# One transformer layer on eight cores: an earlier weight load, two input loads on another queue, an earlier reload for the second half, and a down projection moved behind the next chunk

## The chip, the cores and the metric

The kernel runs on one Trainium2 chip. It is one program on all 8 cores; each core takes one of the 8 sequences of the batch and computes the whole layer for it. The cores exchange nothing. The metric is the device time in microseconds of the slowest core.

## What is computed

One layer, post-layernorm: linear attention with a gate, then a mixture of 16 experts with a shared expert, each followed by residual and layernorm. Per core: 2048 tokens of width 1024, all float32.

```python
q = elu(x @ Wq + bq) + 1;  k = elu(x @ Wk + bk) + 1;  v = x @ Wv + bv     # 16 heads of 64
kv   = einsum('bhsd,bhse->bhde', k, v)          # one 64x64 matrix per head, over all 2048 tokens
attn = q @ kv
h    = layernorm(x + (sigmoid(x @ Wg + bg) * attn) @ Wo + bo)
c    = top-4 of 16 gate weights of softmax(h @ gate_w.T), within the best 2 of 4 groups
y    = sum over experts e of c[:, e] * ((silu(h @ w1[e]) * (h @ w3[e])) @ w2[e])    # inner width 512
z    = (silu(h @ ws1) * (h @ ws3)) @ ws2                                            # inner width 1024
out  = layernorm(h + y + z)
```

## The kernel before

Every float32 operand of a large matmul is split in two bf16 parts (hi and lo), and each product is three matmuls, hi x hi, hi x lo and lo x hi, which the helper `mm3s` (lines 238 to 243) issues. So all large matmuls stand at lines 239, 241 and 242, whatever they compute.

The program is a list of operations per engine (`Sched`, lines 51 to 85), unrolled in full. Each operation has waits on semaphores (an engine's counter and a value), each engine runs its list strictly in order, and a DMA is started by the engine in whose list it stands: "sy" is SyncE (the trace's SPq), "gp" is GpSimd (POOL), "se" is ScalarE (ACT). `Sched.add` drops a wait that the same engine has already made with at least that value.

Stages, in order of time:

- Phase A (lines 263 to 357), 16 tiles of 128 tokens: k and v, and their product kv in PSUM. Then kv is copied out of PSUM on VectorE (line 365), cast on ScalarE (369), and its low part computed on VectorE (370).
- The weights of phase B, Wq, Wg, Wo (386 to 403), in 12 chunks through the single staging buffer `wstage`: DMA on SyncE's queue (390), cast to hi on ScalarE (397), lo part on GpSimd (399). The next chunk's load waits for the lo part of the one before. The first chunk's load waits for `barA`, the last operation of phase A on TensorE, VectorE and ScalarE.
- Phase B (441 to 639), 8 chunks of 256 tokens: load x (445, SyncE's queue, two loads of 512 KB into one of two buffers `xb`), transpose (458), q, g, attention, Wo, residual, layernorm, h written to DRAM (`h_scr`, and transposed as `hth_scr` and `htl_scr`). The x loads of chunks 0 and 1 stand in SyncE's list behind the twelve weight loads.
- Phase C (726 to 1095), two halves `hh` of 1024 tokens. Each half: 16 loads of the transposed h (732, 736), zero `acc` (740), router (757 to 859), 16 experts (861 to 970) with weights staged by `load_split_slot`, then the shared expert, then the layernorm `LN` (1062 to 1092).

Shared expert: its weights ws1, ws3, ws2 come in 12 chunks through `wstage` (972 to 990): load on SyncE's queue (977), a copying DMA on GpSimd's queue for the hi part (983), the lo part on GpSimd (986). For each group of 512 tokens (`tg` 0 and 1) it runs over 8 inner chunks `ic` (994). Each `ic` is 24 + 24 matmuls for h1 (ws1) and h3 (ws3), then silu on ScalarE (1013), product on VectorE (1017), cast (1021) and low part (1025). After `ic` 3 and after `ic` 7 the down projection of the four chunks just made follows: 96 matmuls with ws2 into PSUM banks 4 to 7, eight results of 512 columns, each added to `acc` on VectorE (1052). Here y0 is the one after `ic` 3 and y1 the one after `ic` 7. The buffer `aT` holds four chunks only, so `ic` 4 may write it only after y0 has read it.

LN, eight tiles of 128 tokens: load of h on ScalarE's queue into the single buffer `hln` (1063), residual on VectorE (1066), sums and scaling (1071 to 1086), output written by a DMA that stands in GpSimd's list (1090). For the second half the lists go on: SyncE's has the 16 loads of the transposed h (they wait for `pe_gate`, all of TensorE's work of the first half), then the first expert's weights; GpSimd's has the eight output DMAs of LN ahead of the first expert's copying DMA (718) and lo part (720); VectorE's has LN ahead of the zeroing (740) and of the router's copies (777).

Of the kernel before, what the change touches and what calls it, by code (L numbers as in the profile page):

```python
# [22 lines left out]
ALU = mybir.AluOpType  # L23
# [64 lines left out]
def build_program():  # L88
    nc = bass.Bass("TRN2", target_bir_lowering=False)

    xin = nc.dram_tensor("x", [S, D], F32, kind="ExternalInput").ap()
# [22 lines left out]

    Sd = Sched()
    for nm in ("PE", "VE", "SE", "GP", "GPD", "LDI", "LDB", "XA0", "XA1", "WA",
               "XB0", "XB1", "WB", "HW", "HTW", "HT", "HR", "OUT", "SWL", "WSH"):
        Sd.sem(nm)

    bfree = {i: None for i in range(8)}  # L120

    with ExitStack() as ctx:
# [4 lines left out]
        pb = [ctx.enter_context(nc.psum_tensor("pb%d" % i, [128, 512], F32))  # L127
              for i in range(8)]
# [32 lines left out]
        for t in range(2):  # L161
            xa_pre[t] = Sd.dma("sy", lambda e, t=t: e.dma_start(
                out=PA[:, t * 1024:(t + 1) * 1024], in_=xin[t * 128:(t + 1) * 128, :]),
                inc="XA%d" % t)
# [18 lines left out]
        def bias_col(b_hbm, dest):  # L183
# [39 lines left out]
        stage_free = None  # L223
        for half in range(4):
            for wi, hbm in ((0, wk_h), (1, wv_h)):
                ev_l = Sd.dma("sy", lambda e, hbm=hbm, half=half: e.dma_start(
                    out=wstage.rearrange("p (c i) -> p c i", c=2),
                    in_=hbm[half * 256:(half + 1) * 256].rearrange("(c p) i -> p c i", p=128)),
                    waits=[stage_free], inc="WA")
# [33 lines left out]
        for t in range(NT):  # L263
            p = t % 2
            if t < 2:
                xa_ready[p] = xa_pre[t]
            else:
                xa_ready[p] = Sd.dma("sy", lambda e, t=t, p=p: e.dma_start(
                    out=xa[p], in_=xin[t * 128:(t + 1) * 128, :]),
                    waits=[xa_free[p]], inc="XA%d" % p)  # L270
            ev_xT = [None, None]
            for bi in range(2):
                ev_tr = None
                for j in range(4):
# [7 lines left out]
                    waits=[ev_tr, xT_free[p]])  # L282
# [99 lines left out]
        wo_hi = PW[:, 16384:20480].bitcast(BF16)  # L382
        wo_lo = PW[:, 20480:24576].bitcast(BF16)
        wb_ev = [[None] * 4, [None] * 4, [None] * 4]
        stage_free_b = barA + ([stage_free] if stage_free else [])
        for wi, hbm in ((0, wq_h), (1, wg_h), (2, wo_h)):
            hi = (wq_hi, wg_hi, wo_hi)[wi]
            lo = (wq_lo, wg_lo, wo_lo)[wi]
# [40 lines left out]

        xb_free = [[barA_pe, a_ve_tail], [barA_pe, a_ve_tail]]  # L430
        xb_ready = [None, None]
        xTb_cons = None
        qT_cons = None
        ga_cons = None
# [5 lines left out]

        for cc in range(NCH):
            p = cc % 2
            ev = None
            for st2 in range(2):
                ev = Sd.dma("sy", lambda e, cc=cc, st2=st2, p=p: e.dma_start(
                    out=xb[p][:, st2 * 1024:(st2 + 1) * 1024],
                    in_=xin[cc * 256 + st2 * 128: cc * 256 + (st2 + 1) * 128, :]),
                    waits=[xb_free[p]], inc="XB%d" % p)
            xb_ready[p] = ev

            ev_xtev = []
            for wv_i in range(4):
# [237 lines left out]
        shared_lo = [PW[:, k * 8192 + 4096:(k + 1) * 8192].bitcast(BF16) for k in range(3)]  # L690

        half_end_bar = list(barB)
        hln_free = None
        res2_guard = None
        out_guard = None
# [28 lines left out]
            return ev_lo  # L724

        for hh in range(2):
            pe_gate = list(barB) if hh == 0 else [("PE", Sd.cnt["PE"])]
            ve_gate = list(barB) if hh == 0 else [("PE", Sd.cnt["PE"]), ("VE", Sd.cnt["VE"])]
            out_gate = None if hh == 0 else ("OUT", Sd.cnt["OUT"])
            ev_ht = None  # L730
# [261 lines left out]
            for tg in range(2):  # L992
                a_evs = []
                for ic in range(8):
                    b1i = 0 if ic % 2 == 0 else 2
                    b3i = 1 if ic % 2 == 0 else 3
                    ev_h1 = None
                    ev_h3 = None
                    for c in range(8):
                        mh = hTm_hi[:, c * 1024 + tg * 512: c * 1024 + tg * 512 + 512]  # L1000
                        ml = hTm_lo[:, c * 1024 + tg * 512: c * 1024 + tg * 512 + 512]
                        s1h = shared_hi[0][:, c * 1024 + ic * 128: c * 1024 + ic * 128 + 128]
                        s1l = shared_lo[0][:, c * 1024 + ic * 128: c * 1024 + ic * 128 + 128]
                        ev_h1 = mm3s(pb[b1i][:, :], s1h, s1l, mh, ml, c == 0, c == 7,
                                     [sh_rdy[0], ev_ht, bfree[b1i]], want=(c == 7))
                    for c in range(8):
                        mh = hTm_hi[:, c * 1024 + tg * 512: c * 1024 + tg * 512 + 512]
                        ml = hTm_lo[:, c * 1024 + tg * 512: c * 1024 + tg * 512 + 512]
                        s3h = shared_hi[1][:, c * 1024 + ic * 128: c * 1024 + ic * 128 + 128]
                        s3l = shared_lo[1][:, c * 1024 + ic * 128: c * 1024 + ic * 128 + 128]  # L1010
                        ev_h3 = mm3s(pb[b3i][:, :], s3h, s3l, mh, ml, c == 0, c == 7,
                                     [sh_rdy[1], ev_ht, bfree[b3i]], want=(c == 7))
                    ev_sh = Sd.se(lambda e, b1i=b1i: e.activation(
                        out=sh1b, in_=pb[b1i][:, :], func=AF.Silu),
                        waits=[ev_h1, sh1_guard])
                    bfree[b1i] = ev_sh
                    ev_a = Sd.ve(lambda e, b3i=b3i: e.tensor_tensor(
                        out=aTf, in0=sh1b, in1=pb[b3i][:, :],
                        op=ALU.mult), waits=[ev_sh, ev_h3, aT_cons, h3c_guard, aTf_guard])
                    bfree[b3i] = ev_a  # L1020
                    ev_ahi = Sd.se(lambda e, ic=ic: e.copy(
                        out=aT_hi[:, (ic % 4) * 512:((ic % 4) + 1) * 512],
                        in_=aTf),
                        waits=[ev_a, aT_cons])
                    ev_alo = Sd.ve(lambda e, ic=ic: e.tensor_tensor(
                        out=aT_lo[:, (ic % 4) * 512:((ic % 4) + 1) * 512],
                        in0=aTf,
                        in1=aT_hi[:, (ic % 4) * 512:((ic % 4) + 1) * 512], op=ALU.subtract),
                        waits=[ev_ahi, aT_cons])
                    sh1_guard = ev_a  # L1030
                    h3c_guard = ev_a
                    aTf_guard = ev_alo
                    a_evs.append(ev_alo)
                    if ic % 4 == 3:
                        icg = ic // 4
                        for t128 in range(4):
                            yb0 = 4 + ((t128 + icg) % 2) * 2
                            for hf in range(2):
                                bidx = yb0 + hf
                                ev_y = None  # L1040
                                for ic2 in range(4):
                                    sh = aT_hi[:, ic2 * 512 + t128 * 128: ic2 * 512 + t128 * 128 + 128]
                                    sl = aT_lo[:, ic2 * 512 + t128 * 128: ic2 * 512 + t128 * 128 + 128]
                                    icc = icg * 4 + ic2
                                    mh = shared_hi[2][:, icc * 1024 + hf * 512: icc * 1024 + (hf + 1) * 512]
                                    ml = shared_lo[2][:, icc * 1024 + hf * 512: icc * 1024 + (hf + 1) * 512]
                                    ev_y = mm3s(pb[bidx][:, :], sh, sl, mh, ml,
                                                ic2 == 0, ic2 == 3,
                                                a_evs[icg * 4:] + [sh_rdy[2], bfree[bidx]],
                                                want=(ic2 == 3))  # L1050
                                stl = tg * 4 + t128
                                ev_acc = Sd.ve(lambda e, stl=stl, hf=hf, bidx=bidx: e.scalar_tensor_tensor(
                                    out=acc[:, stl * 1024 + hf * 512: stl * 1024 + (hf + 1) * 512],
                                    in0=pb[bidx][:, :], scalar=1.0,
                                    in1=acc[:, stl * 1024 + hf * 512: stl * 1024 + (hf + 1) * 512],
                                    op0=ALU.mult, op1=ALU.add),
                                    waits=[ev_y, ev_acc0])
                                bfree[bidx] = ev_acc
                        aT_cons = ev_y
# [88 lines left out]
```

How the kernel before makes its waits and increments, by code:

```python
def build_program():  # L88
# [999 lines left out]
                    op1=ALU.mult), waits=[ev_rs, out_guard])  # L1088
                res2_guard = ev_o
                out_guard = Sd.dma("gp", lambda e, st=st, hh=hh: e.dma_start(
                    out=out_h[hh * 1024 + st * 128: hh * 1024 + (st + 1) * 128, :],
                    in_=outt), waits=[ev_o], inc="OUT")
            half_end_bar = [("PE", Sd.cnt["PE"]), ("VE", Sd.cnt["VE"]),
                            ("SE", Sd.cnt["SE"]), ("OUT", Sd.cnt["OUT"])]
        out_total = Sd.cnt["OUT"]
        Sd.add("gp", lambda e: e.wait_ge(sems["OUT"], out_total))
        with nc.Block() as block:
            def mk(engname):
                def run(eng):
                    for fn, ws, inc, n in Sd.ops[engname]:
                        for s_, v_ in ws:
                            eng.wait_ge(sems[s_], v_)
                        ins = fn(eng)
                        if inc is not None:
                            ins.then_inc(sems[inc], n)
```

## Time and profile before

| what | us |
|---|---|
| median of the two runs shown | 7121.18 |
| the two runs | 6723.16 and 7519.19 |
| the profiled execution, its own time | 6724.85 |
| its span on the slowest core (core 6) | 6723.3 |
| spans of the eight cores | 6708.2 to 6723.3 |

The two runs lie 12% apart. The profiled execution agrees with the shorter one to 0.03%, so everything read below from the trace belongs to the shorter time. The span is the time from the first to the last instruction of a core; 1.5 us of the profiled execution's time lie outside it. In the rows below a time is in us from the span's start, unless marked ns. PE is TensorE, DVE VectorE, ACT ScalarE, POOL GpSimd, SP SyncE; a "q" behind the name is the queue in which it starts DMAs. The granted clock (PEclk) is the share of TensorE's full speed: 1.00 is 2.4 GHz, 0.50 is 1.2 GHz.

### The profile page before, as it was taken

The page shows a single profiled execution, that of the slowest core. Times are in us where ns is not written, and L with a number is a line of the kernel's source. Part 1 is how long each engine was busy: PE and PEld are TensorE (multiplying, and loading weights), DVE is VectorE, ACT ScalarE, POOL GpSimd, SP SyncE. Part 2 cuts the span into 40 slices and gives each one's busy share as a digit, 9 for nine tenths or more (in the row PEclk, how much of TensorE's full clock was granted, in tenths as well). Part 3 has the DMA queues.
Part 4 walks back from the last instruction along what each step waited for, and adds up shares of the span by engine and source line. Part 5 has one row for each costly group of instructions (what it writes and reads, how often), then busy time and mean ns, then how long its engine had stood idle before and what let it go on. Part 6 is the DMA issues. An engine that isn't in the chain of part 4 may idle for free.

```text
span 6723.3 us, 66786 instructions; the slowest of 8 cores (6708.2 to 6723.3 us)
## 1 busy us (share of the span) xinstructions
PE 5708.3 (85%) x27750; PEld 2741.6 (41%) x27750; DVE 1711.5 (25%) x2464; ACT 690.2 (10%) x1126; POOL 1143.2 (17%) x608
## 2 busy tenths in 40 slices
PE   3885487875999999999999584899999999999585
PEld 1442364552444444444444232344444444444232
DVE  2221133332222222222222013222222222222113
ACT  1111222221000000000000001000000000000001
POOL 0001111011321221221220200321122122121210
PEclk9897687886999999999999797899999999999798
DMA  2001111002422322232230303432233222221211
GB/s 70 19 16 35 59 35 37 21 32 85 111 74 62 83 82 57 79 83 65 69 83 21 94 10 94 113 85 72 61 84 82 57 79 82 66 69 47 66 38 50
DMA packets 149088, 425.00 MB, mean 63 GB/s; under 512 B 11155, under 2 KB 11427, under 8 KB 148662
## 3 DMA queue, kind: packets, MB, share of 16 engines
q1 hardware_dynamic: 106678, 273.91, 12.2%
q0 software_dynamic: 39808, 138.44, 9.6%
q10 hardware_dynamic: 2304, 8.39, 0.4%
q8 instruction: 222, 3.64, 0.2%
q14 instruction: 76, 0.62, 0.0%
HBM read 282.28 MB, written 25.17 MB: 46 GB/s over the span
## 4 chain that ended last, share of the span: by engine, by line
PE 80%; DMA 7%; DVE 6%; POOL 3%; ACT 2%; issue 2%; SPq 0%; DVEq 0%; ACTq 0%; POOLq 0%
PE pb L239 26%; PE pb L241 26%; PE pb L242 26%; DMA PW<-PW 2%; DMA PW<-ws 2%; POOL PW L986 1%; DVE PM L944 1%; DMA PS<-h_scr 1%; PE pb L868 1%; DMA PW<-w 1%; POOL PW L720 1%; POOL PW L399 1%; DVE PM L951 0%; DVE PA L543 0%; ACT PA L547 0%
## 5 line engine op out<-in xcount | busy, mean ns | idle before, releaser
L239 PE MATMUL pb<-PA,PW 128*128 128x512 bf16 (+1 forms) x5632 | 2040.1, 362 | 187.6 <-POOL PW L986 153.1
L241 PE MATMUL pb<-PA,PW 128*128 128x512 bf16 (+1 forms) x5632 | 2039.4, 362 | 0.0
L242 PE MATMUL pb<-PA,PW 128*128 128x512 bf16 (+1 forms) x5632 | 2038.2, 362 | 0.0
L239 PE MATMUL pb<-PW,PM 128*128 128x512 bf16 x2304 | 889.0, 386 | 125.3 <-DVE PM L951 54.8
L720 POOL TENSOR_TENSOR PW<-PW 128x2048 bf16<-128x2048 f32 x192 | 786.4, 4096 | 742.5 <-DMA PW<-PW 742.5
L241 PE MATMUL pb<-PW,PM 128*128 128x512 bf16 x2304 | 889.5, 386 | 0.0
L242 PE MATMUL pb<-PW,PM 128*128 128x512 bf16 x2304 | 887.6, 385 | 0.0
L239 PEld LDWEIGHTS pb<-PA,PW 128*128 128x128 bf16 x5632 | 554.7, 98 | 777.0 <-issue 227.2
L939 DVE TENSOR_TENSOR PM<-pb,PM 128x512 f32<-128x512 f32 x256 | 177.1, 692 | 2514.9 <-PE pb L242 2514.9
L242 PEld LDWEIGHTS pb<-PA,PW 128*128 128x128 bf16 x5632 | 555.0, 99 | 563.2 <-issue 8.8
L241 PEld LDWEIGHTS pb<-PA,PW 128*128 128x128 bf16 x5632 | 554.5, 98 | 556.9 <-issue 7.2
L718 POOL DMA_DIRECT2D PW<-PW x192 | 111.3, 580 | 2250.2 <-PE pb L242 1310.7
L908 DVE SCALAR_TENSOR_TENSOR PA<-pb,PA 128x512 f32<-128x512 f32 x512 | 339.2, 692 | 357.7 <-PE pb L242 356.7
L239 PE MATMUL pb<-PW,PA 128*128 128x512 bf16 x768 | 314.7, 410 | 111.1 <-DVE PA L283 95.3
L239 PEld LDWEIGHTS pb<-PW,PM 128*128 128x128 bf16 x2304 | 228.5, 99 | 420.0 <-issue 160.2
L935 ACT ACTIVATE PM<-pb 128x512 f32<-128x512 f32 x256 | 153.0, 598 | 2102.8 <-PE pb L242 2102.7
L242 PEld LDWEIGHTS pb<-PW,PM 128*128 128x128 bf16 x2304 | 228.8, 99 | 282.1 <-issue 17.9
L241 PEld LDWEIGHTS pb<-PW,PM 128*128 128x128 bf16 x2304 | 228.3, 99 | 276.5 <-issue 15.7
L947 ACT CAST PM<-PM 128x512 bf16<-128x512 f32 x256 | 158.5, 619 | 1730.0 <-DVE PM L944 1730.0
L241 PE MATMUL pb<-PW,PA 128*128 128x512 bf16 x768 | 313.3, 408 | 0.0
L242 PE MATMUL pb<-PW,PA 128*128 128x512 bf16 x768 | 311.2, 405 | 0.0
L944 DVE TENSOR_TENSOR PM<-PM 128x512 f32<-128x512 f32 x256 | 291.4, 1138 | 26.6
(145 smaller groups left out, 2394.9 us busy)
## 6 DMA issues: line engine op xcount, KB each, us to landing
PW<-w SPq DMA_DIRECT2D x192, 1024.0 KB, 5.2
PW<-PW POOLq DMA_DIRECT2D x216, 512.0 KB, 4.2
PW<-ws SPq DMA_DIRECT2D x24, 1024.0 KB, 5.0
PA<-x SPq DMA_DIRECT2D x32, 512.0 KB, 3.9
h_scr<-PA POOLq DMA_DIRECT2D x16, 512.0 KB, 3.0
PS<-h_scr ACTq DMA_DIRECT2D x16, 512.0 KB, 3.5
out<-PM POOLq DMA_DIRECT2D x16, 512.0 KB, 2.9
PW<-Wk SPq DMA_DIRECT2D x4, 1024.0 KB, 4.8
```

Of the source, the lines that this page charges most:

```text
L239: Sd.pe(lambda e: e.matmul(bk_ap, sh, mh, start=first, stop=False), waits=waits0, want=False)
L241: Sd.pe(lambda e: e.matmul(bk_ap, sh, ml, start=False, stop=False), want=False)
L242: return Sd.pe(lambda e: e.matmul(bk_ap, sl, mh, start=False, stop=last), want=want)
L399: ev_lo = Sd.add("gp", lambda e, hi_ap=hi_ap, lo_ap=lo_ap: e.tensor_tensor(out=lo_ap, in0=wstage, in1=hi_ap, op=ALU.subtract), waits=[ev_h ...
L718: ev_hi = Sd.dma("gp", lambda e, hi_ap=hi_ap: e.dma_start(out=hi_ap, in_=wstage), waits=[ev_l, slot_free[kind][par]], inc="GPD")
L720: ev_lo = Sd.add("gp", lambda e, hi_ap=hi_ap, lo_ap=lo_ap: e.tensor_tensor(out=lo_ap, in0=wstage, in1=hi_ap, op=ALU.subtract), waits=[ev_h ...
L868: cb_mm.append(Sd.pe(lambda e, e_i=e_i, hf=hf, cbk=cbk: e.matmul(pb[cbk][:, :], onehot[0:16, e_i * 128:(e_i + 1) * 128], cT[:, hf * 512:(h ...
L908: ev_acc = Sd.ve(lambda e, stl=stl, hf=hf, bidx=bidx: e.scalar_tensor_tensor(out=acc[:, stl * 1024 + hf * 512: stl * 1024 + (hf + 1) * 512 ...
L935: ev_sh = Sd.se(lambda e: e.activation(out=sh1b, in_=pb[0][:, :], func=AF.Silu), waits=[ev_h1, sh1_guard, out_gate])
L939: ev_h3c = Sd.ve(lambda e, par=par, tg=tg: e.tensor_tensor(out=h3cb, in0=pb[1][:, :], in1=cbuf[par][:, tg * 512:(tg + 1) * 512], op=ALU.mult),
L944: ev_a = Sd.ve(lambda e: e.tensor_tensor(out=aTf, in0=sh1b, in1=h3cb, op=ALU.mult), waits=[ev_sh, ev_h3c, aT_cons, aTf_guard])
L947: ev_ahi = Sd.se(lambda e, ic=ic: e.copy(out=aT_hi[:, ic * 512:(ic + 1) * 512], in_=aTf), waits=[ev_a, aT_cons])
```

## The change

1. The load of the first Wq chunk no longer waits for `barA`, only for the staging buffer's last use in phase A. The cast that reads it still waits for TensorE's last work of phase A.
2. The x loads of phase B's chunks 0 and 1 (four DMAs of 512 KB) leave SyncE's list. They are issued from GpSimd's list, behind the twelve lo parts (399), with semaphores of their own. Chunks 2 to 7 stay on SyncE's queue.
3. For the second half the 16 loads of the transposed h wait only for the last h3 matmul of the first half, not for all of its matmuls. VectorE's gate `ve_gate` is as before.
4. In the shared expert y0 is issued after the h1 and h3 matmuls of `ic` 4, ahead of the operations of `ic` 4 on ScalarE and VectorE. y1 stays behind `ic` 7.

```diff
-        stage_free_b = barA + ([stage_free] if stage_free else [])
+        stage_free_b = [stage_free] if stage_free else []
 ...
         xb_free = [[barA_pe, a_ve_tail], [barA_pe, a_ve_tail]]
         xb_ready = [None, None]
+        xb_pre = [None, None]
+        for cc0 in range(2):
+            ev = None
+            for st2 in range(2):
+                ev = Sd.dma("gp", lambda e, cc0=cc0, st2=st2: e.dma_start(
+                    out=xb[cc0][:, st2 * 1024:(st2 + 1) * 1024],
+                    in_=xin[cc0 * 256 + st2 * 128: cc0 * 256 + (st2 + 1) * 128, :]),
+                    waits=[barA_pe, a_ve_tail], inc="XBP%d" % cc0)
+            xb_pre[cc0] = ev
 ...
         for cc in range(NCH):
             p = cc % 2
-            ev = None
-            for st2 in range(2):
-                ev = Sd.dma("sy", ...  waits=[xb_free[p]], inc="XB%d" % p)
-            xb_ready[p] = ev
+            if cc < 2:
+                xb_ready[p] = xb_pre[cc]
+            else:
+                ... as before
 ...
-            pe_gate = list(barB) if hh == 0 else [("PE", Sd.cnt["PE"])]
+            pe_gate = list(barB) if hh == 0 else [sh_h_last]
 ...
                         ev_h3 = mm3s(pb[b3i][:, :], s3h, s3l, mh, ml, c == 0, c == 7, ...)
+                    sh_h_last = ev_h3
+                    if ic == 4:
+                        icg = 0
+                        for t128 in range(4):
+                            ... the 96 matmuls of y0 and their eight additions to acc
+                        aT_cons = ev_y
                     ev_sh = Sd.se(... Silu ...)
 ...
                     a_evs.append(ev_alo)
-                    if ic % 4 == 3:
-                        icg = ic // 4
+                    if ic == 7:
+                        icg = 1
                         for t128 in range(4):
```

## Rows read from the trace of the kernel before

**Rows 1.** The page: the span and TensorE's busy time, share, instructions.

```profile
span 6723.3 us, 66786 instructions; the slowest of 8 cores (6708.2 to 6723.3 us)
PE 5708.3 (85%) x27750; PEld 2741.6 (41%) x27750; DVE 1711.5 (25%) x2464; ACT 690.2 (10%) x1126; POOL 1143.2 (17%) x608
```

**Rows 2.** The page: the chain that ended last, share by engine.

```profile
PE 80%; DMA 7%; DVE 6%; POOL 3%; ACT 2%; issue 2%; SPq 0%; DVEq 0%; ACTq 0%; POOLq 0%
```

**Rows 3.** Waits, whole span: waiter, what it waited for, us, times, longest.

```profile
PE pb L239 <- POOL PW L986: 188.7, 6, 48.6
PE pb L458 <- DMA PA<-x: 141.6, 1, 141.6
```

**Rows 4.** The chain in time, end of phase A: start, us, what.

```profile
611.28 1.05 ACT PM L369
...
613.79 5.40 DMA PW<-Wq
619.32 1.91 ACT PW L397
```

**Rows 5.** The same chain where phase B begins.

```profile
738.15 0.46 SPq L445
738.66 9.76 DMA PA<-x
```

**Rows 6.** Timeline there, GpSimd: start, us, instruction [idle before it].

```profile
746.82 4.06 POOL L399 TENSOR_TENSOR PW<-PW 128x2048 bf16<-128x2048 f32 x1 [9.15 <-ACT PW L397]
```

**Rows 7.** The page's DMA issues: count, size, median us to landing.

```profile
PW<-PW POOLq DMA_DIRECT2D x216, 512.0 KB, 4.2
...
PA<-x SPq DMA_DIRECT2D x32, 512.0 KB, 3.9
```

**Rows 8.** Timeline of VectorE, shared expert, first half, `tg` 0, from `ic` 3.

```profile
3867.07 0.69 DVE L1017 TENSOR_TENSOR PM<-PM,pb 128x512 f32<-128x512 f32 x1 [8.17 <-PE pb L242]
...
3890.85 0.69 DVE L1052 SCALAR_TENSOR_TENSOR PA<-pb,PA 128x512 f32<-128x512 f32 x1 [19.30 <-PE pb L242]
...
3908.98 0.69 DVE L1052 SCALAR_TENSOR_TENSOR PA<-pb,PA 128x512 f32<-128x512 f32 x1 [1.90 <-PE pb L242]
3919.48 0.69 DVE L1017 TENSOR_TENSOR PM<-PM,pb 128x512 f32<-128x512 f32 x1 [9.81 <-PE pb L242]
...
3929.84 0.69 DVE L1017 TENSOR_TENSOR PM<-PM,pb 128x512 f32<-128x512 f32 x1 [8.17 <-PE pb L242]
```

**Rows 9.** Timeline of GpSimd, first half: the last chunk of ws2.

```profile
3881.34 4.04 POOL L986 TENSOR_TENSOR PW<-PW 128x2048 bf16<-128x2048 f32 x1 [3.72 <-DMA PW<-PW]
```

**Rows 10.** Windows: stretch, its us, busy by engine, PEclk, DMA share, GB/s.

```profile
3843.00:3860.00 17.00, 17.00 (x81) 7.65 (x80) 2.77 (x4) 1.84 (x3) 4.64 (x2) 1.00 0.42 119
...
3867.00:3885.50 18.50, 0.00 (x0) 0.00 (x0) 3.68 (x2) 0.62 (x1) 8.63 (x3) 0.58 0.30 85
3885.50:3890.85 5.35, 5.32 (x14) 1.96 (x15) 0.00 (x0) 0.00 (x0) 0.00 (x0) 0.53 0.00 0
```

**Rows 11.** Timeline of VectorE, second half, `tg` 0: `ic` 3, then y0.

```profile
6426.25 0.69 DVE L1017 TENSOR_TENSOR PM<-PM,pb 128x512 f32<-128x512 f32 x1 [8.17 <-PE pb L242]
...
6447.82 0.69 DVE L1052 SCALAR_TENSOR_TENSOR PA<-pb,PA 128x512 f32<-128x512 f32 x1 [18.39 <-PE pb L242]
```

**Rows 12.** Waits of TensorE, 3900 to 4103 (columns as in rows 3).

```profile
PE pb L239 <- DVE PM L1025: 7.7, 3, 2.6
```

**Rows 13.** Windows: LN of the first half, LN of the second.

```profile
4103.66:4174.47 70.81, 1.85 (x64) 1.79 (x64) 32.29 (x57) 12.86 (x25) 3.78 (x7) 0.54 0.57 185
6660.63:6718.79 58.16, 0.00 (x0) 0.00 (x0) 32.29 (x57) 12.86 (x25) 3.78 (x7) 0.54 0.39 136
```

**Rows 14.** Waits in 3705 to 4270, TensorE.

```profile
PE pb L767 <- DVE PM L777: 52.1, 1, 52.1
PE pb L767 <- DMA PA<-htl_scr: 25.8, 1, 25.8
```

**Rows 15.** Windows: inside the first half's LN.

```profile
4120.00:4125.00 5.00, 0.00 (x0) 0.00 (x0) 2.00 (x2) 0.79 (x1) 0.00 (x0) 0.50 1.02 347
```

More of the change, by code:

```diff
@@ L116, in build_program @@
     for nm in ("PE", "VE", "SE", "GP", "GPD", "LDI", "LDB", "XA0", "XA1", "WA",
-               "XB0", "XB1", "WB", "HW", "HTW", "HT", "HR", "OUT", "SWL", "WSH"):
+               "XB0", "XB1", "XBP0", "XBP1", "WB", "HW", "HTW", "HT", "HR",
+               "OUT", "SWL", "WSH"):
         Sd.sem(nm)
@@ L442, in build_program @@
             p = cc % 2
-            ev = None
-            for st2 in range(2):
[L445 to L448, printed above, removed]
-            xb_ready[p] = ev
+            if cc < 2:
+                xb_ready[p] = xb_pre[cc]
+            else:
+                ev = None
+                for st2 in range(2):
+                    ev = Sd.dma("sy", lambda e, cc=cc, st2=st2, p=p: e.dma_start(
+                        out=xb[p][:, st2 * 1024:(st2 + 1) * 1024],
+                        in_=xin[cc * 256 + st2 * 128: cc * 256 + (st2 + 1) * 128, :]),
+                        waits=[xb_free[p]], inc="XB%d" % p)
+                xb_ready[p] = ev
             ev_xtev = []
@@ L692, in build_program @@
         half_end_bar = list(barB)
+        sh_h_last = None
         hln_free = None
@@ L1012, in build_program @@
                                      [sh_rdy[1], ev_ht, bfree[b3i]], want=(c == 7))
+                    sh_h_last = ev_h3
+                    if ic == 4:
+                        icg = 0
+                        for t128 in range(4):
+                            yb0 = 4 + ((t128 + icg) % 2) * 2
+                            for hf in range(2):
+                                bidx = yb0 + hf
+                                ev_y = None
+                                for ic2 in range(4):
+                                    sh = aT_hi[:, ic2 * 512 + t128 * 128: ic2 * 512 + t128 * 128 + 128]
+                                    sl = aT_lo[:, ic2 * 512 + t128 * 128: ic2 * 512 + t128 * 128 + 128]
+                                    icc = icg * 4 + ic2
+                                    mh = shared_hi[2][:, icc * 1024 + hf * 512: icc * 1024 + (hf + 1) * 512]
+                                    ml = shared_lo[2][:, icc * 1024 + hf * 512: icc * 1024 + (hf + 1) * 512]
+                                    ev_y = mm3s(pb[bidx][:, :], sh, sl, mh, ml,
+                                                ic2 == 0, ic2 == 3,
+                                                a_evs[icg * 4:] + [sh_rdy[2], bfree[bidx]],
+                                                want=(ic2 == 3))
+                                stl = tg * 4 + t128
+                                ev_acc = Sd.ve(lambda e, stl=stl, hf=hf, bidx=bidx: e.scalar_tensor_tensor(
+                                    out=acc[:, stl * 1024 + hf * 512: stl * 1024 + (hf + 1) * 512],
+                                    in0=pb[bidx][:, :], scalar=1.0,
+                                    in1=acc[:, stl * 1024 + hf * 512: stl * 1024 + (hf + 1) * 512],
+                                    op0=ALU.mult, op1=ALU.add),
+                                    waits=[ev_y, ev_acc0])
+                                bfree[bidx] = ev_acc
+                        aT_cons = ev_y
                     ev_sh = Sd.se(lambda e, b1i=b1i: e.activation(
```

## The prediction

> **What bounds the kernel now.** I first read the page's head: TensorE is busy for 85% of the span [rows 1]. The chain that ended last says the same of the path: 80% of it is TensorE, the rest is mostly DMA and VectorE [rows 2]. So the kernel is matmul time plus the places where TensorE stands still, and this change takes no matmul away (the 27750 stay). It can gain only in those places. The waits show which they are: 188.7 us on the lo parts of the shared weights, in six waits, and one of 141.6 us for the first x load of phase B [rows 3]. Then I took three stretches in order of time: the chain from phase A to phase B [rows 4, 5], the shared expert [rows 8 to 12], and LN of the first half [rows 13 to 15]. What ends last is a different thing in each, so each edit is priced in its own stretch.
>
> **Edits 1 and 2, the start of phase B.** Before, the kv cast on ScalarE ends at 611.28 + 1.05 = 612.3. VectorE's last operation follows, then the first Wq load, issued at 613.79 and 5.40 us long, and its cast starts at 619.32 [rows 4]. In the changed kernel that load has landed long before, and its cast is next on ScalarE behind the kv cast: it starts at 612.4, or 6.9 us earlier. From there twelve chunks hand one buffer on, each cast, lo part, load. So all the later chunks move forward by 6.9 us. This is the whole gain of edit 1, and it reaches TensorE only if the x load moves forward too.
>
> Edit 2 decides that. Before, SyncE issued the x loads at once behind the last weight load, at 738.15, while the last cast and lo part (to 746.82 + 4.06 = 750.9) were still to come. The first chunk's x came at 738.66 + 9.76 = 748.4, and with it TensorE's start [rows 5, 6]. After, the same loads stand in GpSimd's list behind the last lo part. Queued ahead of them is thus exactly the work which they passed before. The last weight load is issued about 737.7 - 6.9 = 730.8 and has the DMA engines to itself, so I give it 5.2 us, a little under the 5.40 of the first [rows 4]: it lands at 736.0. Cast 1.9 and lo part 4.06 with 0.2 of hand-over end at 742.1. Four issues follow, about 0.5 us apart (an estimate from the step between 738.15 and 738.66, which is SyncE's). The second x load of chunk 0 is issued at 742.7. The trace has no x load on this queue. The bounds are 3.9 us (the median of x loads on SyncE's queue) and 9.8 us (the load of rows 5, which shared the engines); the nearest row is the 512 KB copy on GpSimd's own queue, 4.2 us [rows 5, 7]. With a second load just ahead I take 4.7 us: landing 747.4 against 748.4 before. Edits 1 and 2 together give 1 us, between a gain of 2 and a loss of 4. The 6.9 us are lost behind the lo part. The other weights are no new wait, since q needs only Wq, ready long before.
>
> The Trainium skill ("DMA: Bandwidth & Descriptors", section "Issuing engine by pattern") speaks against edit 2: a plain load belongs on SyncE, and the path through GpSimd is generally the slower one. Its section "Anatomy of one DMA — SWDGE (gpsimd) path" prices such a DMA at 2.0 us plus bytes over 436 GB/s, by which the first MB would take an estimated 4.4 us instead of my 4.7, and the sum would move by 0.3 us. No row here shows an HBM load on that queue.
>
> **Edit 4, `tg` 0 of both halves.** The h3 matmuls of `ic` 3 end where its product starts, 3867.07. y0 then waits, not for that product, but for the last lo part of ws2, which ends at 3881.34 + 4.04 = 3885.4 [rows 8, 9]. TensorE does nothing for 18.5 us [rows 10]. Then come y0 (last addition starts at 3908.98) and the 48 matmuls of `ic` 4, until 3919.48 [rows 8]. One `ic` costs 3929.84 - 3919.48 = 10.36 us. In the changed kernel these 48 matmuls need only ws1 and ws3, which are there, and PSUM banks 0 and 1, free since `ic` 2. They run inside the gap, from 3867.1 to 3877.4, and y0 still starts at 3885.5. So 10.36 us are taken out behind y0. In the second half the product of `ic` 3 starts at 6426.25 and the first result of y0 is there at 6447.82, about 5.3 us after its start, so at 6442.5 [rows 11]: the gap is 16 us, and 10.36 fit again. Together 20.7 us.
>
> **Edit 4, `tg` 1.** The weights are there, and y0 waits for product, cast and low part of `ic` 3. The first half has three such waits between 3900 and 4103, 7.7 us in all: y1 of `tg` 0, y0 and y1 of `tg` 1, 2.6 us each [rows 12]. Only y0's goes, covered by the 10.36 us of `ic` 4. Twice 2.6 is 5.2 us. What is late next: `ic` 4's product now waits until y0 has read `aT`, and VectorE has y0's eight additions first. That chain takes some 3 us behind y0 and its bank is wanted only by `ic` 6, 10.4 us behind y0. It costs nothing. ScalarE's cast of `ic` 4 holds up the silu of `ic` 5, which comes 5.2 us after y0's end, later than that cast.
>
> The clock: after the gap the granted clock is 0.53, and the first result takes 3885.50 to 3890.85, 5.35 us, against (3908.98 - 3890.85) / 7 = 2.59 for each later one [rows 8, 10]. So 2.8 us are paid on resuming. In the changed kernel the gap is 8 us (6 in the second half). I charge the same 2.8 again. If the clock stayed up it would be 2 x 2.8 = 5.6 us more gain.
>
> **Edit 3.** Its direct aim, TensorE's wait of 25.8 us for the transposed h, is worth nothing: the next row is 52.1 us of the same router matmuls waiting for VectorE, which has LN ahead of them, and GpSimd has LN's output DMAs ahead of the first expert's weights [rows 14]. LN sets the end of this stretch. But the 16 loads run beside it. LN of the first half takes 70.81 us, with 185 GB/s moving; LN of the second, the same work with no such loads, 58.16. In both VectorE's work is 32 us [rows 13]; the difference is h loads that crawl while the DMA engines are full, at share 1.02 and 347 GB/s [rows 15]. With the loads gone from LN it takes what the second does: 70.8 - 58.2 = 12.6 us less, and router and first weights follow at once. Are they gone? They can start 23.3 us before LN (the wait of 2.6 and eight results of 2.59). To move are 4.2 MB and the first expert's 1.05 MB, 5.25 MB: 15 us at 347 GB/s, 28 us at the 185 GB/s of LN's mean. At the lower bound a fifth of the burst still lies in LN and keeps 2.5 of the 12.6. I take all 12.6. Under the burst y1 runs; matmuls ran without loss at clock 1.00 beside a DMA share of 0.42, the nearest row [rows 10]. What it costs at share 1.0 no row shows; bounds are nothing and the 12.6 us that it saves.
>
> **Sum.** 1.0 + 20.7 + 5.2 + 12.6 = 39.5 us, against the profiled execution's own 6724.85: 6685 us, 0.6% less. Of the two runs shown that execution matches the faster (6723.16). Their median, 7121.18, is the middle of two runs 12% apart and no base for a sum of microseconds.
>
> **Rivals.**
> (a) The x loads come late. GpSimd's queue moves all four as one stream, and chunk 0 takes the 9.8 us of rows 5: landing at 752.5, 4 us after the old time. For it: a lone row of 4.2 us is for one copy, and here are four. Against: the engines have nothing else to do. 5 us worse: 6690. Chance 0.14.
> (b) The burst isn't hidden: y1 or the first LN tiles lose what LN gains. For it: all eight cores pull 5 MB at once, and no row has a full DMA load beside full matmuls. Against: all eight cores run the same program, and core 6 still got 347 GB/s [rows 15]. Edit 3 gives 0: 6698. Chance 0.12.
> (c) The shorter gaps leave the clock up, and x lands a little sooner: 39.5 + 5.6 + 1: 6679. For it: the gaps are 8 and 6 us instead of 18 and 16. Against: in the row the clock has gone down on the mean of the gap already (0.58, of which 0.50 is the floor, so it was down for most of it). Chance 0.09.
> (d) The other side. y0 runs at the lower clock through. The two short bursts, `ic` 4 in the old gap and y0 behind a new one, do not bring the clock back after 5 us as in rows 10. All of y0 at 1.2 GHz costs 8 x 2.59 = 20.7 us instead of 2.8, so 17.9 more, in each half 35.8. Gains are then 3.7; it is slower than before (6726 or more) once the lower clock reaches 2 us into `ic` 5 in each half. Against: y0 is the same dense stream as before. Chance 0.02.
> (e) The change doesn't do what it says: an unseen wait keeps y0 or the loads where they were. Every wait in the code is as told above, so 0.02, about 6710.
>
> **Numbers.** The forecast, 6685, has chance 0.61, its own range is 6678 to 6692. (a) 0.14, (b) 0.12, (c) 0.09, (d) 0.02, (e) 0.02. The range for 8 in 10 reaches from below (c), with both ends of the unknown costs, to past (b): 6670 to 6702. A difference of 2%, 134 us, is about what a measurement of this kernel can tell from no change. The largest gain that the terms allow is 2 + 20.7 + 5.2 + 5.6 + 12.6 = 46 us. So faster by over 2%: 0.01; slower by over 2%: 0.02, for a clock or contention effect that no row shows; within 2%: 0.97.
>
> **What would show each step.** Edit 1: the first cast (397) near 612.4, idle before it under 1 us. Edit 2: the first transpose (458) at 747 to 748, not at 741.6, with the lo parts ended at 742; if x lands under 745 or over 750, my load price is wrong. Edit 4: in each `tg` 0 TensorE idle about 8 and 6 us ahead of y0, with 48 more matmuls before it; the waits on L1025 go from three to two per half. Edit 3: LN of the first half near 58 us, its h loads at 3.1 to 3.6 us each; the wait of L767 on the transposed h gone, that on VectorE longer. The prediction fails if matmuls in y1 slow down under the loads, if a gap between phases moves that I haven't priced, or if the total moves by more than these rows add up to.

## The result

The changed kernel takes 0.9942 of the time before (95% interval 0.992 to 0.9965): the change gains about half a percent. The median of the changed kernel's 33 executions is 6757.59 us, that of the 32 before 7109.94. In half or more of the executions of either kernel the cores of one die or of both get a lower TensorE clock; both medians mix these with the others, and all comparisons here leave such executions and cores out. What is left are 17 executions of the changed kernel, 6691 to 6722 us with a median of 6698.9 (one of them is not among the 33), and nine of the kernel before, 6723 to 6732 us with a median of 6729.2. So the change saves about 30 us, where I had summed 39.5.

The cores of the changed kernel's profiled execution:

```profile
core 6: 6686.1 us, clock 0.923
...
die 0 (median of its cores): 6751.3 us, clock 0.913
die 1 (median of its cores): 6686.5 us, clock 0.923
```

So I read cores 4 to 7 of it, and core 6 for rows, as before. The lines of this kernel's file have moved: the weight cast is line 398, its lo part 400, the x transposes 471, the matmuls of `mm3s` 240 to 243. Four readings answer the four steps. First the start of phase B, the chain in order of time (start, us, what):

```profile
612.22 1.90 ACT PW L398
...
737.52 3.93 issue
741.45 0.69 POOL PA L437
742.15 5.74 DMA PA<-x
748.02 1.10 PE pb L471 x4
```

The first cast of Wq starts at 612.22, 7.1 us sooner than in [rows 4]. The last lo part (in the chain's piece "issue") is done at 741.5, nine us sooner than in [rows 6]. The x load is issued behind it (line 437), and the first transpose starts at 748.02, half a microsecond sooner than in [rows 5]. The head start is gone.

Second, the gap ahead of y0, windows of core 6 (us, busy of PE, PEld, DVE, ACT, POOL, then PEclk, DMA share, GB/s):

```profile
3867.80:3878.30 10.50, 10.14 (x48) 4.39 (x45) 3.78 (x2) 1.22 (x2) 4.63 (x2) 1.00 0.26 100
3878.30:3885.80 7.50, 0.00 (x0) 0.00 (x0) 0.00 (x0) 0.00 (x0) 4.03 (x1) 0.72 0.36 70
3885.80:3891.35 5.55, 5.38 (x13) 1.90 (x14) 0.00 (x0) 0.00 (x0) 0.02 (x1) 0.50 0.01 3
```

The 48 matmuls of `ic` 4 fill the first part of the old gap of [rows 10]; 7.5 us stay idle, and y0 still resumes at clock 0.50.

Third, LN of the first half, from y1's last addition to the start of LN's last scaling plus its 0.8 us:

```profile
4094.57:4151.64 57.07, 1.49 (x60) 1.40 (x56) 32.20 (x57) 12.86 (x25) 3.78 (x7) 0.55 0.38 138
```

70.81 in [rows 13] has become 57; the DMA share is 0.38, as in the second half. Fourth, TensorE's waits, 3690 to 4240 of core 6 (us in all, times, longest):

```profile
PE pb L240 <- POOL PW L1000: 85.6, 3, 49.0
PE pb L781 <- DVE PM L791: 64.6, 1, 64.6
...
PE pb L240 <- DVE PM L1066: 5.2, 2, 2.6
```

The wait for the transposed h is gone, and the one for VectorE behind it is 12.5 us longer, against [rows 14]; so the early reload gave TensorE nothing by itself. The waits on the low part (line 1066 here) are two instead of three [rows 12].

### The profile page after: what moved, and what is told of

Same layout as the page of the kernel before. It is cut to its first block, busy times and chain, and to the rows that moved or that the text cites. A ratio compares the mean times of both kernels' runs of the same rounds, so it can differ in the third digit from the quotient of the medians.

```text
span 6756.1 us, 66786 instructions; the slowest of 8 cores (6675.6 to 6756.1 us)
## 1 busy us (share of the span) xinstructions
PE 5765.4 (85%) x27750; PEld 2756.8 (41%) x27750; DVE 1742.8 (26%) x2464; ACT 688.3 (10%) x1126; POOL 1141.5 (17%) x612
## 3 DMA queue, kind: packets, MB, share of 16 engines
q1 hardware_dynamic: 106102, 271.82, 12.1%
## 4 chain that ended last, share of the span: by engine, by line
PE 80%; DMA 7%; DVE 6%; POOL 3%; ACT 2%; issue 2%; DVEq 0%; SPq 0%; ACTq 0%; POOLq 0%
PE pb L240 26%; PE pb L242 26%; PE pb L243 26%; DMA PW<-PW 2%; DMA PW<-ws 2%; POOL PW L1000 1%; DVE PM L958 1%; PE pb L882 1%; DMA PW<-w 1%; DMA PS<-h_scr 1%; POOL PW L734 1%; POOL PW L400 1%; DVE PM L965 1%; DVE PA L556 0%; ACT PA L560 0%
## 5 line engine op out<-in xcount | busy, mean ns | idle before, releaser
L240 PE MATMUL pb<-PW,PA 128*128 128x512 bf16 x768 | 334.8, 436 | 114.6 <-DVE PA L284 98.9
L242 PE MATMUL pb<-PW,PA 128*128 128x512 bf16 x768 | 334.1, 435 | 0.0
L243 PE MATMUL pb<-PW,PA 128*128 128x512 bf16 x768 | 332.3, 433 | 0.0
```

## Eight cores instead of one

The prediction was worked out on core 6. For the experiments I cut each core's work at the same places and took the mean; the number of cores is in brackets. The places are starts, read from each core's timeline: the first cast of Wq (A), the first x transpose (B), the row of expert 15's last two additions in either half (C), the last addition of the shared expert (D), LN's last scaling (E). So C to D is the shared expert, and D to E is LN. All in us.

```
kernel (cores)              A      B     A to C   C to D  D to E   C to D  D to E   last E
                                         1st half 1st     1st      2nd     2nd
before (8)                617.4  744.0   3122.9   361.5    66.6    357.8    56.8    6710.8
changed (4)               610.9  745.8   3130.6   348.9    56.4    346.8    57.0    6679.7
e1 edit 4 alone (8)       615.8  741.7   3123.6   349.3    65.9    347.5    57.1    6687.9
e2 edit 3 alone (4)       614.7  740.9   3120.1   361.2    58.0    358.7    56.8    6699.4
e3 edits 1+2 alone (8)    610.7  745.7   3131.5   360.6    65.2    357.7    57.0    6712.2
e4 without edit 2 (8)     607.8  734.2   3125.0   350.0    56.5    346.6    57.1    6671.4
e5 edit 2 alone (8)       620.5  754.5   3137.2   360.1    67.0    357.3    56.4    6728.6
e6 x ahead (8)            610.2  610.6   3122.5   348.6    57.1    346.4    57.1    6670.9
e7 interleaved (8)        608.2  608.0   3079.8   347.9    56.7    347.3    57.0    6624.7
e8 y1 covered too (8)     608.5  743.4   3134.6   346.8    57.2    343.7    56.7    6676.0
e10 y0 behind ic 5 (8)    610.6  745.4   3129.3   338.7    57.3    337.8    56.3    6658.0
e12 one x (4)             610.7  744.1   3137.8   349.6    56.2    344.9    57.5   6690.7
e11 all (2)               610.9  610.7   3077.8   333.3    56.7    332.4    56.2    6598.8
e13 all, again (8)        607.5  607.2   3078.5   333.9    57.8    332.7    56.8    6595.4
```

A itself varies by some 5 us from one execution to the next, since phase A does; so B is compared through B minus A. What edit 1 does to A itself is read from a place that phase A's length does not blur, the start of the kv cast on ScalarE: A comes 7.64 us behind it in the kernel before and 0.95 us behind it with edit 1, and B 134.2 us in the kernel before, 135.8 in the changed kernel, 127.3 in e4.

## The experiments

**e1, edit 4 alone** (the changed kernel with edits 1 to 3 undone).

> Edit 4 alone (y0 behind the matmuls of ic 4), edits 1 to 3 undone. My theory: it shortens the stretch from the last addition of expert 15 to the first half's LN from 361.4 us (mean of the eight cores before) to about 349 and the same stretch of the second half from 357.7 to about 347, and touches nothing else: LN of the first half stays at 64 to 70 us from its start to its last output scaling, the x load stays. 23 us less in all, ratio 0.9965. Rival (the clock): y0's shift makes the wait of 2.6 us ahead of y1 cost 1.5 us more in a good part of the cases (the first result of y1 6.7 us behind the product of ic 7 instead of 5.2), because the clock falls in it; then that shows here too, with the other edits gone. If those dips are chance, they come as rarely here as before (3 of 32).

Measured: ratio 0.9962 (0.9948 to 0.9975). The shared stretches are 12.2 and 10.3 us shorter, LN stays at 65.9. Each half lacks a part of the 13.0 that I had priced (10.36 of the gap and 2.6 of the wait in `tg` 1), and the rival tells most of why. Rows of core 6 of the changed kernel show a case. First the timeline of VectorE (`ic` 7's product, y1's first addition), then windows:

```profile
3941.02 0.69 DVE L1058 TENSOR_TENSOR PM<-PM,pb 128x512 f32<-128x512 f32 x1 [8.17 <-PE pb L243]
...
3947.70 0.69 DVE L1093 SCALAR_TENSOR_TENSOR PA<-pb,PA 128x512 f32<-128x512 f32 x1 [4.48 <-PE pb L243]
```

```profile
3941.00:3943.50 2.50, 0.14 (x1) 0.14 (x2) 1.38 (x2) 0.62 (x1) 0.00 (x0) 0.89 0.00 0
3943.50:3945.00 1.50, 1.50 (x4) 0.45 (x3) 0.00 (x0) 0.00 (x0) 0.00 (x0) 0.50 0.04 11
3945.00:3947.00 2.00, 2.00 (x8) 0.80 (x7) 0.00 (x0) 0.00 (x0) 0.00 (x0) 0.65 0.00 0
```

The wait is the old 2.6 us, but the clock falls in it to 1.2 GHz and comes back in the third stretch, so the first result comes 6.68 us behind the product, not 5.19. In e1 17 of the 32 waits ahead of y1 show such a lag of over 6.4 us. In the kernels without edit 4 (before, e2, e3, e5) it is 6 of 168 waits of the same length, all six ahead of `tg` 0's y1; ahead of `tg` 1's y1 it is none of 56 there and 11 of 16 in e1. So the dip isn't chance, and no other edit is needed for it to be frequent. Against the kernel before the dips cost 2.8 of the missing 3.5 us. The other 0.8 lies in the second half, where y0 itself came that much later behind `ic` 3's product; the changed kernel shows 0.3 there.

**e2, edit 3 alone.**

```diff
-            pe_gate = list(barB) if hh == 0 else [("PE", Sd.cnt["PE"])]
+            pe_gate = list(barB) if hh == 0 else [sh_h_last]
```

> Edit 3 alone (the reload of the transposed h waits only for the last h3 matmul). My theory: LN of the first half falls from a mean of 66.6 us over the cores to 56.5, the value of the second half, on every core, and y1 under the burst keeps its 18.1 us from first to last addition; 10 us less in all, ratio 0.9985. Rival, that I overrated it: I read the 12.6 us on core 6, where LN was slowest (70.0 us); the gain of the slowest core is then less than the 12.6 that I predicted, since the cores' times vary for other reasons too. Rival (b) of the prediction: the burst slows y1 or LN's first tiles, and the total doesn't move.

Measured: ratio 0.9986 (0.9968 to 1.0004). LN of the first half falls to 58.0 us on cores 4 to 7, 8.6 less than before's mean, and the stretch with y1 in it takes 361.2 against 361.5. (A comes 2.7 us sooner and B to C is 2.4 us shorter, where edit 3 does nothing: such is the spread of one execution.) So y1 runs at full speed under the burst, here read on core 7 (VectorE, y1's first and last addition, 18.13 us apart, as the same rows are in the kernel before):

```profile
4085.80 0.69 DVE L1055 SCALAR_TENSOR_TENSOR PA<-pb,PA 128x512 f32<-128x512 f32 x1 [3.00 <-PE pb L243]
...
4103.93 0.69 DVE L1055 SCALAR_TENSOR_TENSOR PA<-pb,PA 128x512 f32<-128x512 f32 x1 [1.90 <-PE pb L243]
```

A window of the same core, within y1, shows the burst beside it (columns as above):

```profile
4086.00:4095.00 9.00, 9.00 (x43) 4.08 (x42) 2.57 (x4) 0.00 (x0) 0.00 (x0) 1.00 0.95 327
```

TensorE is busy all the time at clock 1.00, beside a DMA share of 0.95 and 327 GB/s. The four cores take 18.13 us each, and so do all eight of the kernel before. The mechanism holds, rival (b) of the prediction falls. What the size of the gain hangs on is the wait for h, whole LN, VectorE. First core 6 before (the row is within 4103.7 to 4174.5), then core 6 of the changed kernel:

```profile
DVE PM L1066 <- DMA PS<-h_scr: 27.9, 8, 6.2
```

```profile
DVE PM L1107 <- DMA PS<-h_scr: 14.5, 8, 2.6
```

It fell by 13.4 us on that core. But before, LN took 64.1 to 70.0 us over the cores, and core 6 had the 70.0.

**e3, edits 1 and 2 alone.**

> Edits 1 and 2 alone. My theory: the first cast of Wq moves from 619.3 to 612.3, the last lo part from 750.9 to 741.5, and the first transpose of phase B stays between 742 and 750, as before (739 to 749 over the cores): ratio 1.000, within 0.0005. The rival of who meant the edit as a gain of 7 us: first transpose near 738, ratio 0.999. Rival (a): x on GpSimd's queue lands 9.8 us behind its issue, first transpose at 752, 5 us more.

Measured: ratio 1.0038 (0.9976 to 1.01), no change that can be told. A is 6.7 us sooner and B 1.7 later: B minus A is 135.0 instead of 126.6. Edit 1 does what it says, edit 2 costs 8.4 us. Rival (a) of this run's text, 9.8 us for the load, falls: the second x load of chunk 0 took 4.4 to 5.9 us on the eight cores.

**e4, edit 2 undone** (x back behind the weights on SyncE's queue), **and e5, edit 2 alone.**

> The changed kernel with edit 2 undone: the x loads are back in SyncE's list behind the weight loads, edits 1, 3 and 4 stay. My theory: what edit 1 gains is lost only because x stands behind the last lo part; on SyncE's queue the loads go out at about 731 and land at 741 less the noise, and the first transpose comes at 734 to 742, 6 to 7 us sooner than in the changed kernel. Total 6 us less than the changed kernel, ratio to before 0.993. Rival: the x load's landing is set by the traffic of all cores and not by its place in a list; then the first transpose comes no sooner than in the changed kernel (742 to 750).

> Edit 2 alone: the first Wq load waits as before, the x loads stand in GpSimd's list. My theory: the loss of edit 2 comes without edit 1's 6.7 us, so the first transpose comes at about 752 on the mean of the cores, 135 us behind the first cast of Wq (before: 744 and 127, with the loads on SyncE's queue). Rival: the queue itself costs nothing and x would land as soon as before once the last lo part is not in front; then 129 us or less.

Measured: e4 0.9951 (0.9891 to 1.0011), an interval too wide to tell; the last E comes 8.3 us sooner than in the changed kernel. B minus A is 126.4, as in the kernel before (126.6), and 134.0 in e5, where edit 1 is gone. So the 7 to 9 us hang on the list that the loads stand in. They are the difference of two things: the second x load of chunk 0 is issued 129.9 us behind A in the changed kernel and 118.8 in e4, 11 us later, and it then takes 4.8 us instead of 7.4 (means of the cores). The chain of e4, core 6:

```profile
724.49 0.37 SPq L391
725.02 0.35 SPq L446
725.41 6.62 DMA PA<-x
732.17 1.10 PE pb L459 x4
```

x goes out right behind the last weight load, 118.3 us behind this core's A of 607.1, where in the changed kernel it was 129.9, and beside that weight load takes 6.62 us instead of 5.74.

**e12, only chunk 0's loads on GpSimd.**

> The changed kernel, but only chunk 0's two x loads stand in GpSimd's list; chunk 1's are back on SyncE's queue behind the last weight load, where nobody waits for them. My theory: in the changed kernel chunk 0's x shares the engines with chunk 1's, 2 MB in one burst; alone its 1 MB lands about 1.5 us sooner: the first transpose 133 to 134 us behind the first cast instead of 135. Rival: the landing is fixed cost of the queue, and it stays at 135.

B minus A is 133.4 us (four cores), 1.5 less than in the changed kernel. That is the number of my theory, but not by its mechanism: the last lo part ended 128.1 us behind A instead of 129.3, which is 1.2 of the 1.5, and the load itself took 4.5 us instead of 4.8. So the second chunk's MB costs chunk 0 at most 0.3 us, and the rival, a landing that does not hang on the other MB, is nearer to what the rows show. The 8 us are the place behind the last lo part.

**e6, x ahead of eleven weight loads.**

```diff
+                if wi == 0 and half == 0:
+                    ... the four x loads of chunks 0 and 1, on SyncE, waits=[barA_pe, a_ve_tail]
```

> The changed kernel with the x loads of chunks 0 and 1 back on SyncE's queue, but right behind the first Wq load, ahead of the other eleven. My theory: the start of phase B is then no longer set by x, but by ScalarE, which has all twelve casts of weights in its list ahead of its first work on x. The first transpose comes at 616 to 622 instead of 742 to 750, and the first q matmul about 3 us behind the twelfth cast's end (735 to 741), 13 us sooner than in the changed kernel. Total 13 us less than the changed kernel, ratio to before 0.993. Rival: phase B's start is bound by the weights themselves; then an early x brings nothing against the run with x on SyncE's queue behind the weights, and no more than 8 us against the changed kernel.

Measured: ratio 0.9896 (0.981 to 0.9982). The last E is 8.8 us sooner than in the changed kernel, not 13, and level with e4: my number fell and the rival's held. On core 6 x is there for the first transpose at 612.5, but ScalarE's list lets nobody use it (timeline of ScalarE, core 6):

```profile
735.74 1.90 ACT L408 CAST PW<-PW 128x2048 bf16<-128x2048 f32 x1 [9.58 <-DMA PW<-Wo]
737.54 1.07 ACT L479 CAST PA<-pb 128x512 bf16<-128x512 f32 x2
740.24 0.59 ACT L479 CAST PA<-pb 128x512 bf16<-128x512 f32 x1 [1.63 <-PE pb L472]
```

The first cast of x (479) follows the twelfth weight cast (408). In e4 the x of core 6 lands at 732.0, only 0.6 us behind the end of its twelfth cast (731.4), so an earlier x could win hardly anything.

**e7, the weight chunks handed out within chunk 0**: `wload(k)` issues chunk k; k = 1 to 3 behind the transposes, 4 to 7 behind every second q result, 8 to 11 behind every second g result; x ahead as in e6.

> As the run with x ahead, and the weight chunks are handed out within chunk 0: Wq's four around the transposes, Wg's four between the q results, Wo's four between the g results. Same work. My theory: q and g of chunk 0 (42 us of matmuls) and the transposes run while Wg and Wo are still coming, and the attention of chunk 0 starts right behind the last Wo cast at about 741. The stretch from the first kv cast to expert 15 of the first half gets 50 to 60 us shorter than in the changed kernel; ratio to before 0.986. Rival: each cast now waits in ScalarE's list behind q and g operations, so the chain of twelve chunks gets longer by what it gives; then less than half of the 50 us appear.

A to C is 50.8 us shorter than in the changed kernel, the last E 55 us sooner. There is no interval for it; the one execution that counts took 6645.7 us. The rival falls: the chain of twelve chunks did get longer, by 4.5 us (its last lo part ends 133.8 us behind A on the mean, against 129.3), but not by half of the 50. Windows of core 6, the kernel before and then e7:

```profile
700.00:748.00 48.00, 0.00 (x0) 0.00 (x0) 0.00 (x0) 7.60 (x4) 17.41 (x5) 0.50 0.35 116
```

```profile
700.00:745.00 45.00, 22.46 (x167) 17.56 (x165) 6.11 (x7) 11.50 (x14) 16.24 (x4) 0.73 0.21 71
```

TensorE worked 22 us in a stretch in which it had stood still. This is where the 141.6 us of [rows 3] were to be had; the wait's releaser, the x load, was only the last of the things in front of the work: the casts in ScalarE's list stood there too, and the chain of weight loads that feeds them.

**e8, y1 of `tg` 0 behind the matmuls of `tg` 1's `ic` 0.**

> The changed kernel, and y1 of tg 0 stands behind the matmuls of ic 0 of tg 1, so its wait of 2.6 us is covered as y0's was. My theory: 2.6 us less in each half, and the loss of 1.5 us by the clock that y1 of tg 0 has in a third of the cases goes with it: the shared stretch of both halves gets 3 us shorter, total 6 us less, ratio to before 0.9945. It also tells on the clock: only the wait ahead of the last y1 is left. If the clock's dip there comes from a long dense stretch ahead of it, it comes in every case now, in both halves (first result 6.8 us behind the product); if it comes from where the wait falls in time, its share changes either way.

Ratio 0.9925 (0.987 to 0.9981). The shared stretches are 2.1 and 3.1 us shorter than in the changed kernel. My theory had 3 us for each half. Of the last y1's waits 12 of 16 show the dip: not all, so a long dense stretch ahead isn't its cause, at least not alone.

**e10, y0 behind the matmuls of `ic` 5 as well.**

> The changed kernel, and y0 stands behind the matmuls of ic 5 as well as ic 4. My theory: these 10.4 us fill what is left of the gap ahead of y0 in tg 0 (8 us in the first half, 6 in the second), so the lower clock on resuming (2.8 us) goes too: the shared stretch gets 10 us shorter in the first half and 9 in the second, total 19 us less than the changed kernel, ratio to before 0.9925. In tg 1 nothing changes. Rival: the operations of ic 4 and ic 5 on ScalarE and VectorE now come in one heap behind y0 and hold up the banks that ic 6 needs: then TensorE waits ahead of ic 6 or 7 by up to 5 us in each tg, and half of the gain is lost.

Ratio 0.9891 (0.9815 to 0.9967). The shared stretches are 10.2 and 9.0 us shorter than in the changed kernel, the priced 10 and 9. TensorE's waits, 3860 to 4100 of core 6, in the changed kernel and in e10:

```profile
PE pb L240 <- POOL PW L1000: 8.0, 1, 8.0
PE pb L240 <- DVE PM L1066: 5.2, 2, 2.6
```

```profile
PE pb L240 <- DVE PM L1075: 5.2, 2, 2.6
```

The gap is gone (on all eight cores and in both halves the first result of y0 comes 23.17 us behind `ic` 3's product, which is about two `ic` and one result of matmuls), and there is no new wait for banks, so the rival falls. The dip came in 15 of the 16 waits ahead of `tg` 0's y1 and in 8 of 16 ahead of `tg` 1's.

**e11 and e13, all that gained, twice the same kernel.**

> All that gained, together: the changed kernel with the interleaved start, y0 behind the matmuls of ic 5, and y1 of tg 0 behind those of ic 0 of tg 1. My theory: the gains lie in separate stretches and add up. Against the changed kernel the end of the work (mean of the cores, 6679.7 us) comes 55 us sooner for the start, 10 and 9 for y0, and about 5 for y1 in all: about 6602 us, ratio to before 0.984. Rival: y0's and y1's moves share one gap and one clock dip, so together they give no more than y0's move alone (19): 6606 to 6608.

> The version with all that gained, once more, for an execution with all eight cores undisturbed: two cores of the first one ended their work at 6598.8 us on the mean, 112 less than before's mean. If that holds on all eight, the spans lie at 6595 to 6612 us, the time at 6610 to 6618, ratio to before 0.983. If the two cores were a lucky draw, the other cores lie at 6615 and above.

The gains add up. The last E comes at 6598.8 (two cores) and 6595.4 us (all eight), 115 us sooner than before. The shared stretches of e13 are 15.0 and 14.1 us shorter than in the changed kernel, no less than e10's and e8's gains together (12.3 and 12.1), so the rival falls. The spans of e13 lie at 6589 to 6607; its two executions that count took 6608.93 and 6609.12 us, against 6722 to 6732 for five of the kernel before beside them, so about 0.982 (two against five, and no interval). One window of core 6 shows TensorE where the gap of [rows 10] was:

```profile
3860.00:3895.00 35.00, 35.00 (x164) 15.87 (x162) 5.92 (x9) 3.75 (x7) 0.00 (x0) 1.00 0.00 0
```

Of the 16 waits ahead of its last y1, one shows the dip.

## Why the prediction was right and wrong

It was wrong in the number that it named: 6685 us with a range of 6670 to 6702, and the measured median is 6757.6. The step that failed is the base of the sum. The 39.5 us were taken from the profiled execution's own 6724.85, and the median of the two runs was put aside as "no base for a sum of microseconds". I had the sign in hand, two executions 12% apart, and didn't ask where a median of many would fall. Of the changed kernel's 33 executions 16 took 6691 to 6722 us, and the median is the next above them; had one more been as short, it would have been 6722 or less. Of the 32 before only nine took less than 6740, and their median is 7109.94. So where the median falls hangs on the mix and not on the waits that were summed, and the range should have reached well past 6702 for that alone.

Against the executions of the profiled kind the mechanisms were right in the main, but the sum was too large: 39.5 us for 30, or for 31.1 by the mean of the cores. The median of the 17, 6698.9, is inside the range and outside the forecast's own 6678 to 6692. That it is rival (b)'s 6698 is chance, since what (b) says didn't happen (e2). It is also partly luck that 0.6% less agrees so well with the ratio's 0.58%; by the medians 6729.2 and 6698.9 it is 0.45%. That the change stays within 2% held. Step by step:

- **Edit 1**: right. Measured from the kv cast, the first cast moved by 6.7 us on the mean of the cores (forecast 6.9), and the gain got lost behind the last lo part, as told.
- **Edit 2**: wrong in sign, though inside its own bounds (a gain of 2 to a loss of 4). Forecast 1 us of gain for both edits; measured 1.7 to 1.8 us of loss (B 744.0, then 745.8 in the changed kernel and 745.7 in e3; from the kv cast 1.6 and 1.7). The load's own price held, 5.74 us on core 6 and 4.5 on the other three, against my 4.7, and so did the end of the last lo part (741.5 for 742.1). What failed is the time before: "738.66 + 9.76". On core 6 itself B did move the right way, by 0.5 us, but core 6 had the slowest x load of the eight. Core 5 of the kernel before, its chain:

```profile
733.99 6.53 DMA PA<-x
```

The eight took 6.5 to 9.8, on the mean 7.6. The 2.2 us between are most of the 2.8 by which the term was off.

- **Edit 4, the gap**: right. 10.36 us twice, y0 not later in the changed kernel by more than 0.3 us, 2.8 us paid again on resuming, no bank or list held up. e10 confirmed the price of the rest of the gap.
- **Edit 4, the wait in `tg` 1**: the wait went as told, but edit 4 as a whole measured 12.6 and 11.0 us in the changed kernel, 12.2 and 10.3 in e1, against 13.0. Missing are 2.4 and 3.5 us. The clock dips ahead of y1, about one in two and 1.4 to 1.7 us each, account for them: against the kernel before they come to 2.7 and 2.8 us, and in e1 a later y0 adds 0.8. I had looked for the clock at y0's gap only, where nothing changed; rival (d) had the right cause at the wrong place and far too large.
- **Edit 3**: mechanism right (the burst leaves LN, y1 doesn't feel it, TensorE's own wait is worth nothing), size off. Forecast 12.6, measured 10.2 in the changed kernel and 8.6 in e2. "LN of the first half takes 70.81" was the slowest of eight cores, 70.0 us by cut D to E, where the mean is 66.6; on core 6 alone the gain was 13.7 us.
- **Rivals**: (a) is out, since x landed 4.5 to 5.7 us behind its issue and not 9.8. (b) is out by e2. (c) is out: the clock did fall in the shorter gaps. (e) is out.

The changed kernel: -1.8 at B, +0.6, +12.6, +10.2, -1.1, +11.0, -0.2 for the stretches in order, 31.3 against the 31.1 of the last E. No stretch is left out. About 3, 2.4 and 2.4 us are what the start, LN and the shared expert fell short by.

What stays open is why a wait of one and the same length, 2.6 us, lets the clock fall in one place in nearly every case (15 of 16 in e10) and elsewhere hardly ever (6 of 168, and 1 of 16 in e13). The runs show that its frequency goes with the place in the program and that the length of the wait doesn't decide it; one and the same place goes either way on different cores. No run here moved one such wait by small steps.

## What to carry to other kernels

Before an operation goes to another engine's list, write down what stands ahead of it there: here a load left the queue where it overtook the last weight split and went behind it, and 8 us were lost, more than the 7 that the earlier weight load had won. Where a wait names one releaser, look what would end it next; an early x was worth nothing against e4 until the casts in ScalarE's list had been dealt out as well, and then 43 us more (A to C, e6 to e7). And price a term on all cores of the profiled execution: the slowest core is the slowest because its waits happened to be long, and these are the ones one is tempted to win back. The time of one profiled execution is also no forecast of a median, when the runs shown lie 12% apart.

## What the runs showed of the hardware

After a wait of 2.6 us TensorE came back at 1.2 GHz, costing 1.4 to 1.7 us, in 17 of 32 cases in e1. A burst of 5 MB of loads beside dense matmuls cost them nothing (18.13 us from the first to the last of the eight results of y1 with and without it, at a DMA share of 0.95). Two loads of 512 KB from DRAM on GpSimd's queue had landed 4.3 to 6.1 us behind the issue of the second (changed kernel, e3, e5, e8, e10), with two more behind them; the mean is 4.9. In e6, e7 and e13 the same two loads on SyncE's queue, beside no weight load either, took 4.0 to 7.0 us, on the mean 4.5. So of the 8 us some 0.4 can be the queue's own. By the Trainium skill's page "DMA: Bandwidth & Descriptors" (section "Anatomy of one DMA — SWDGE (gpsimd) path") an estimated 4.4 us go to that MB, so its figure is close at the lower end. The rule of the same page of the Trainium skill (section "Issuing engine by pattern") that plain loads belong on SyncE held here, by 8 us, but nearly all for what stands in the list and not for the path.
